# Gathers issued as soon as a buffer is free, without waiting for points of TensorE's work

## The reference

```python
x = x + _L0_conv_ref(_gn(x), ...)   # group norm, 4-bit activations, 3x3 conv of signs, batch norm, relu
x = x + _L1_conv_ref(_gn(x), ...)   # the spectral step, below
```

```python
xo = g_lt * gather(qltx, qlty) + g_rb * gather(qrbx, qrby) + g_lb * gather(qltx, qrby) + g_rt * gather(qrbx, qlty)
xo = xo.reshape(...)                 # 9 samples a pixel
return conv2d(xo, wc, 1, stride=KS)  # 3x3 over the samples
```

## Time and profile before

| what | value |
|---|---|
| median of three runs | 7875.68 us |
| the profiled execution | 7877.08 us |
| its span, first to last instruction | 7874.9 us |
| mean granted TensorE clock | 0.862 |
| TensorE busy | 5804.1 us, 74% |
| GpSimd busy | 5285.1 us, 67%, 5040 gathers |
| VectorE busy | 4787.2 us, 61% |
| ScalarE busy | 2756.2 us, 35% |
| the chain that ended last | PE 49%, DVE 19%, POOL 12%, issue 10%, ACT 7%, DMA 2% |

### The profile page before, as it was taken

How to read it: one execution, slowest core, us unless ns; L and a number is a source line. 1 busy time by engine, 2 the same in 40 slices (tenths; PEclk the granted TensorE clock), 3 DMA queues, 4 the chain that set the end, 5 groups by cost and what they waited for, 6 DMA issues and landing times.

```text
span 7874.9 us, 106214 instructions
## 1 busy us (share of the span) xinstructions
PE 5804.1 (74%) x33682; PEld 2822.3 (36%) x33682; DVE 4787.2 (61%) x7421; ACT 2756.2 (35%) x5357; POOL 5285.3 (67%) x5044
## 2 busy tenths in 40 slices
PE   3577776878677876788768887687867787676765
PEld 2333333334333433334333433333433343233323
DVE  3366656576566765666655666557656676565641
ACT  2333333334233343334323343333423334232322
POOL 0277767777577766777667776777757776677760
PEclk7789888889888898889888898888988889888887
DMA  2222222222322223222222222222232222312120
GB/s 85 64 71 62 63 72 68 65 82 63 94 60 64 74 71 81 62 72 67 74 72 65 81 64 74 67 66 82 63 93 61 64 74 71 81 50 68 51 66 21
DMA packets 424838, 540.91 MB, mean 69 GB/s; under 512 B 310746, under 2 KB 318974, under 8 KB 417646
## 3 DMA queue, kind: packets, MB, share of 16 engines
q0 software_dynamic: 161280, 330.62, 16.0%
q1 hardware_dynamic: 262980, 203.17, 10.0%
HBM read 404.04 MB, written 116.94 MB: 66 GB/s over the span
## 4 chain that ended last, share of the span: by engine, by line
PE 49%; DVE 19%; POOL 12%; issue 10%; ACT 7%; DMA 2%; DVEq 1%; SPq 0%; ACTq 0%; POOLq 0%
PE pair L1049 21%; POOL gath L626 12%; PE ring L987 5%; PE ring L906 4%; PE ps_acc L1023 4%; ACT u L1081 3%; DVE gath L1625 3%; PE ps_def L1070 3%; DVE prod L1613 2%; ACT prod L1281 2%; DVE gath L1630 2%; PE ring L951 1%; PE ring L868 1%; PE ring L852 1%; DVE u L1435 1%
## 5 line engine op out<-in xcount | busy, mean ns | idle before, releaser
L626 POOL DMA_INDIRECT gath<-table_d,idx_all x5040 | 5285.1, 1049 | 2359.1 <-issue 1788.4
L1049 PE MATMUL pair<-clamp_x,tab 128*128 128x392 f32 (+1 forms) x5760 | 2830.7, 604 | 1183.5 <-DVE prod L1613 1176.2
L1613 DVE SCALAR_TENSOR_TENSOR prod<-prod,pair 128x392 f32<-128x392 f32 (+1 forms) x2880 | 1610.6, 570 | 1570.4 <-PE pair L1049 1494.8
L1281 ACT ACTIVATE prod<-ps_y,y_bias 128x392 f32<-128x392 f32 (+1 forms) x2880 | 1481.0, 597 | 2457.0 <-PE ps_acc L1023 2154.9
L1049 PEld LDWEIGHTS pair<-clamp_x,tab 128*128 128x128 f32 x5760 | 1142.5, 220 | 2487.9 <-DVE prod L1613 1751.1
L1625 DVE TENSOR_TENSOR gath<-gath,wgt 128x1152 f32<-128x1152 f32 x560 | 758.9, 1355 | 681.4 <-DMA gath<-table_d,idx_all 674.8
L1081 ACT ACTIVATE u<-ring 128x448 f32<-128x448 f32 (+7 forms) x1376 | 605.2, 479 | 877.1 <-PE ring L894 229.9
L1023 PE MATMUL ps_acc<-prod,w_samp 128*32 128x392 f32 (+1 forms) x5760 | 648.5, 523 | 6.5 <-DVE prod L1613 6.5
L1070 PE MATMUL ps_def<-xt,w_samp 32*32 32x224 f32 x5760 | 324.9, 380 | 223.7 <-DVE xt L1637 223.7
L987 PE MATMUL ring<-u,w 128*32 128x392 f32 x5120 | 457.0, 514 | 22.6 <-ACT u L1081 22.6
L906 PE MATMUL ring<-u,w_off 128*64 128x448 f32 (+1 forms) x2048 | 425.4, 514 | 26.4 <-ACT u L1081 26.4
(11 more groups left out here) (155 smaller groups left out, 4093.0 us busy)
## 6 DMA issues: line engine op xcount, KB each, us to landing
gath<-table_d,idx_all POOLq DMA_INDIRECT x5040
table_d<-u SPq DMA_DIRECT2D x192, 210.0 KB
point_d<-u SPq DMA_DIRECT2D x32, 406.0 KB
u<-point_d SPq DMA_DIRECT2D x32, 406.0 KB
u<-in_x SPq DMA_DIRECT2D x8, 1568.0 KB, 7.4
x_d<-u SPq DMA_DIRECT2D x8, 1568.0 KB, 5.8
xg_d<-u SPq DMA_DIRECT2D x8, 1568.0 KB, 5.3
u<-xg_d SPq DMA_DIRECT2D x32, 392.0 KB
```

Source lines behind the costliest of these rows:

```text
L626: pool.indirect_dma_start(gath[:, k % BUFS, n * CELL:(n + 1) * CELL], None, table_d[:, :], bass.IndirectOffsetOnAxis(idx_all[:, k, n:n + 1 ...
L1049: nc.tensor.matmul(bank[:, 0:size], tab[:, b * NB + br, j * 128:(j + 1) * 128], clamp_x[:, s % 2, 0:size], start=True, stop=True)\
L1281: nc.scalar.activation(prod[:, s % 2, j, 0:size], ps_y[:, 0:size], ACT.Relu, bias=y_bias[:, j:j + 1]).then_inc(relu_ready, 1)
L1613: v.scalar_tensor_tensor(rows, rows, 1.0, bank[:, 0:size], ALU.min, ALU.mult)\
```

## The change

GpSimd waits for no point of TensorE's work any more. Before a slot's nine gathers it waits for its buffer alone (and at slots 0 and 35 of a quad for the indices). The first three slots of a quad no longer wait for four more counts. The functions that work out the points are gone, and since all quads are now the same for GpSimd, its program is one hardware loop over eight quads. No other engine's program is touched.

```diff
-GROUPS, LEAD = 3, 3
-
-def pe_events(has_back, has_front):
...
-def gather_pace(has_back, has_front):
-
-    events, slots, _ = pe_events(has_back, has_front)
-    pace = []
-    for k in range(LEAD, NK):
-        lo, hi = slots[k - LEAD], slots[k - LEAD + 1]
-        row = []
-        for g in range(GROUPS):
-            seen = [e for e in events if e[0] <= lo + g * (hi - lo) / GROUPS]
-            row.append(seen[-1][1:] if seen else None)
-        pace.append(row)
-    return [[None] * GROUPS] * LEAD + pace
...
             pool.wait_ge(zeroed, NT * 16)
-
-            def quad(q, has_back, has_front):
-                pace = gather_pace(has_back, has_front)
...
+            with pool.Fori(0, NQ) as q:
                 for k in range(NK):
                     if k % T == 0:
                         pool.wait_ge(index_done, q * NB + k // T + 1)
                         pool.sem_inc(turn[0], 1)
 
-                    pool.wait_ge(xt_ready, q * NK + (BUFS - LEAD if k < LEAD else 0) + k + 1)
+                    pool.wait_ge(xt_ready, q * NK + k + 1)
                     pool.sem_inc(turn[0], 1)
                     for n in range(TAPS):
-                        point = pace[k][n // (TAPS // GROUPS)]
-                        if n % (TAPS // GROUPS) == 0 and point and point != last:
-                            last = point
-                            if point[0] == "unit":
-                                pool.wait_ge(pair_full[0], q * QUAD_USES + point[1])
-                            else:
-                                pool.wait_ge(ring_full[point[1] % 2], done // 2 + point[1] // 2 + 1)
-                            pool.sem_inc(turn[0], 1)
                         pool.indirect_dma_start(
...
-            quad(0, False, True)
-            with pool.Fori(1, NQ - 1) as q:
-                quad(q, True, True)
-            quad(NQ - 1, True, False)
```

## The result

The changed kernel takes 7640.06 us, the median of four runs (7636.96 to 7645.42 us), against 7876.3 us (7872.92 to 7880.06 us) for the kernel before. The ratio is 0.9703, with a 95% interval from 0.9691 to 0.9715. The forecast was 7635 us. The profiled execution took 7636.96 us with a span of 7634.8 us, 240.1 us less than the span of before.

What follows compares the result with a forecast made beforehand. GpSimd's gathers were taken to set the quads' ends, and to bind the last quad throughout. Terms 26.8 + 141 + 62.7 + 12 = 242.5 us off 7877.1 us gave 7634.6, stated as 7635 us, range 7530 to 7820 us.

Steps and rivals of the forecast that it cites:

- quad 0: First quad, bound by GpSimd: its two long waits for points, 16.8 and 10.0 us, go, 26.8 us.
- quads 1 to 5, with the clock: Ends of these quads: TensorE's wait for xt goes, 28.2 x 5 = 141 us, plus 12 us of TensorE's clock.
- quads 6 and 7: Last quad, bound by GpSimd: its gathers can begin 62.7 us earlier, which includes quad 6's end.
- 859 us of gathers a quad: Quad 3, standing for quads 1 to 6: GpSimd's gather work with gaps, 630 x 1.36, in 935 us.
- what is late next is TensorE itself, and the gain is its wait, not VectorE's 34.5 us: Quad ends: VectorE would finish 34.5 us earlier, before TensorE's own end, so the gain is TensorE's 28.15 us wait.
- The clock: TensorE after the removed idle time at the ends of quads 1 to 5: 0 to 20 us gained, 12 taken.
- The gathers' own time: Gathers getting longer when unpaced: 0 to 50 us in quads 0 and 7, taken as 0.
- The second: Rival, ends of quads 1 to 6: another wait replaces the removed one, only quads 0 and 7 gain; 7816 us, chance 0.07.
- The fourth: Rival, all quads: buffers or index_done hold GpSimd where the points did, no effect; 7877 us, chance 0.04.
- The third: Rival: longer free gathers make GpSimd bind every quad; threshold 1.450 us a gather, 8079 us at 1.49; chance 0.08.
- The first: Rival: VectorE's waits inside quads 1 to 6 count too, 138 us more gain; 7497 us, chance 0.07.
- The items to look for: Signs in the trace after: TensorE's and VectorE's waits, first gather after idx_all, quad about 905 us, gather mean 1.03 to 1.08 us.

Runs made afterwards that it cites:

- experiment 8: The changed kernel run again unchanged, KEEP = 66, beside the other KEEP runs on their chip: 7648.18 us, ratio 0.9717.
- Experiments 1 and 2: Kernel before with points taken away for slots 61 to 69 only: 7659.45 us; with points taken away for slots 0 to 60 only: 7870.29 us.
- Experiment 3: Changed kernel with the hold at a quad's first three slots put back (xt_ready four counts higher), no points: 7655.91 us, ratio 0.9729.
- experiment 5: Changed kernel with a 128x256 GpSimd memset after each slot's gathers, its end waited for before the next slot: 7887.65 us, ratio 1.0023.
- experiment 9: Changed kernel with a memset a slot on two tiles in turn, waiting only for the one before the last: 7724.51 us, ratio 0.9819.
- experiment 6: Changed kernel with KEEP = 64 for 66, two slots more behind a quad's last unit: 7553.15 us, ratio 0.9595.

## Why the prediction was right

The terms against what the starts of the last bursts show (in quads 0, 5 and 7: before 1206.7, 5879.6 and 7652.55 us, after 1181.8, 5703.2 and 7415.26 us):

| term | forecast us | measured us |
|---|---|---|
| quad 0 | 26.8 | 24.9 |
| quads 1 to 5, with the clock | 141 + 12 = 153 | 151.5 |
| quads 6 and 7 | 62.7 | 60.8 |
| behind the last burst | 0 | 2.8 |
| sum | 242.5 | 240.1 |

The prediction's own sum gives 7634.6 - 1.4 = 7633 us and not 7635 us, and its 859 us of gathers a quad are 630 x 1.364; with the 1.36 that it writes they are 857 us. Neither changes the argument. That the forecast lies within 5 us of the result is in part luck: the changed kernel's repetition (experiment 8) took 7648.18 us, and three terms are 1.5 to 1.9 us too high where one that was left out is 2.8 us.

*Quads 1 to 5.* The step "what is late next is TensorE itself, and the gain is its wait, not VectorE's 34.5 us" held, and it is the step that carries the number. Five quads gave 30.3 us each: the wait of 28.35 us (mean of the five) and 2.0 us more. Experiments 1 and 2 show the place. Had the waits in the middle of the quads been counted too, the forecast would have been 138 us lower.

*Quad 0.* It has gained its two long waits for points less 1.9 us. 0.8 us of it is that its first gather came later (339.7 against 338.9 us). TensorE's wait there is still 29.21 us:

```profile
1181.80 5.97 PE L1010 MATMUL ps_def<-xt,w_samp 32*32 32x224 f32 x72 [29.21 <-DVE xt L1577]
```

It was 51.83 us; the forecast said 25 us. It is what a quad without slack leaves: quad 0 is still bound by GpSimd, none of whose gathers there stands idle for more than 0.3 us after the first.

*Quads 6 and 7.* The gather starts 1.1 us behind its indices, and 62.7 us became 60.8 us. Experiment 3 takes 22.5 us of the earlier start away, and its quad 7 loses 15 us: its gathers there take 826.1 us, where the changed kernel's take 835.4 us, and that gives a part back.

*The clock.* 12 us were taken, between 0 and 20 us; the five quads show 151.5 less their waits, 141.7 us, so 9.8 us or 2.0 us a quad. The last burst itself gave 1.7 us of it: over these quads it took 6.12 us on average before and takes 4.40 us after. TensorE's busy time in quads 1 to 6 agrees, before and then after, for the same matmuls 2.4 us less a quad:

```profile
1206.70:6815.60 5608.90, 4323.26 (x25262) 2090.30 (x25263) 3583.75 (x5556) 2062.66 (x4014) 3998.11 (x3781) 0.88 0.28 71
1181.80:6609.40 5427.60, 4309.07 (x25264) 2083.50 (x25264) 3577.22 (x5556) 2065.24 (x4010) 4041.98 (x3804) 0.89 0.29 74
```

The 1.7 us that the prediction took as the bound of the burst were worked out from a row of 4.63 us; the same trace has bursts of 3.61 us, so the bound was 6.12 - 3.61 = 2.5 us, and in quads 1 and 4 after the change the burst takes 3.6 us. That 12 us came near the 9.8 us is a choice within a range that proved right, and no run changed the clock alone.

*The gathers' own time.* Taken as 0 between 0 and 50 us. The row of all gathers answers to the earlier trace rows:

```profile
L571 POOL DMA_INDIRECT gath<-table_d,idx_all x5040: 939/945/3502, 339.7 to 7404.8; - x194
```

The median is 945 ns against 944 ns, the longest 3502 ns against 3323 ns, the mean 3 ns more. The prediction weighed the rule of the Trainium skill (GPSIMD Engine Reference, section 1, Specifications) that GpSimd's SBUF interfaces are shared with VectorE and contend with its instructions of two SBUF inputs. Both traces agree with that rule. The gathers during which VectorE does nothing (1006 before, 905 after) take 944 ns on average, and those that begin within L1553, which reads one input from SBUF and one from PSUM, take 953 ns (L1613 before, 952 ns). Those that begin within L1565, the weighing of a slot with two inputs in SBUF, take 1373 ns (536 gathers), and within L1625 before 1334 ns (524 gathers). So the change made them meet hardly more often. All gathers together take 19 us more (5304.1 against 5285.1 us), and that lies in quads 1 to 6, which have slack; in quads 0 and 7 the means are 1025 and 1017 ns against 1024 and 1019 ns, and there the term is 0 as forecast.

*The other rivals.* The second (another wait at the ends) is refuted by TensorE's timeline, which has none. The fourth (no effect) by the result. The third did not occur, but its threshold did: experiment 5 has 1.454 us a gather and about the time of before, and experiment 9 stayed under it. The slack of 46 us a quad is 0.66 us a slot: the 0.48 us of experiment 9 stay under it and the 0.84 us of experiment 5 go over it, where a quad should take 904 + 59 - 46 = 917 us, and 918 to 923 us were measured. The first is answered by experiments 1 and 2.

*The items to look for.* TensorE's waits (none in quads 1 to 6, 29 for 25 us in quad 0), the first gather right behind idx_all, VectorE's waits (287 for 270 us), the quad (904 for 905 us), the mean gather (1.05 us) and the last quad (1.33 us a gather) all came as said. Of the 287.3 us, 115.8 us lie in quad 0 and 170.4 us in quad 7. GpSimd's waits in quad 3:

```profile
POOL gath L571 <- issue: 202.1, 624, 11.8
POOL gath L571 <- DVE xt L1577: 34.5, 7, 11.2
```

They are for buffers (34.5 us in seven waits) and the indices (11.8 us, under issue). What I did not foresee are the 2.8 us behind the start of the last burst: 1.7 us of them are that burst, 5.29 us before and 3.61 us after, and the rest was not traced further.

## What to carry to other kernels

In this kernel the engine that feeds the others through buffers, and is busy for most of a stage, did best when it waited for its buffer and its inputs alone. Points of progress in another engine's work, set to pace it, cost nothing in the middle of the stage and held it back where its lead was needed, at the end. Look for that where an engine is paced by another's work. Cost a removed stall by the wait at the end of the stage on the engine that is late next, and not by the sum of the waits it caused: 57 us of a quad's waits on VectorE were worth 28 us, and those in its middle nothing. When the stall is gone, try again the numbers that were tuned with it there: KEEP brought 95 us more, of which only 44 were to be had before.

## What the hardware showed that I had not expected

A memset of 128x256 on GpSimd takes 0.33 us, but a gather that waits for its semaphore starts 0.81 us behind it, against 0.30 us behind another gather and 0.16 us behind a memset whose end it doesn't wait for. A wait on the engine's own last instruction costs more here than the instruction. With the short memset the gathers also became longer: of 0.48 us a slot only 0.19 us are the memset and its gaps.

A gather that begins while VectorE weighs a slot takes 1334 ns on average and not 944 ns, but VectorE pays nothing: L1625 takes 1357 ns where gathers run through more than half of it (504 times in the kernel before) and 1349 ns where none does (37 times).

And the granted clock over quads 1 to 6 moved from 0.89 to 0.90 by the order of the work alone (experiment 6 against 8), and with it TensorE's busy time fell by 9.7 of the 17.2 us of a quad's gain.
